# Second layer's weights and first x1 loaded during the first layer, last x1 stores not waited for, and statistics put ahead of the lane product

## What is computed

```python
x = _L0_conv_ref(x, Wk, bk, Wq, bq, Wv, bv, Wp, bp)      # x1, (8, 256, 48, 48)
x = _L1_conv_ref(x, w_qkv, w_dw, w_pw, w_proj, gamma, beta)

# layer 0
keys, queries, values = (conv1x1(x, W, b).reshape(n, 8, 32, hw) for W, b in ...)
context  = einsum('nhkp,nhvp->nhkv', softmax(keys, 3), values)
attended = einsum('nhkv,nhkp->nhvp', context, softmax(queries, 2))
x1 = conv1x1(attended.reshape(n, 256, h, w), Wp, bp) + x

# layer 1
qkv = einsum('oc,bchw->bohw', w_qkv, x1)                 # 768 channels
ms  = depthwise 5x5 (w_dw), then a grouped 8x8 product (w_pw), of qkv
q, k, v1 = relu, relu, v with a row of ones              # 64 heads of 8, of [qkv, ms]
out = (v1 k^T) q;  out = out[:-1] / (out[-1:] + 1e-15)
y   = einsum('oc,bchw->bohw', w_proj, out)
out = (y - mean) * rsqrt(var + 1e-5) * gamma + beta + x1  # mean, var over all images
```

## Time and profile before

| | us |
|---|---|
| median of 3 runs | 2305.25 (2300.67 to 2306.81) |
| profiled execution, its own time | 2298.37 |
| its span in the profile | 2296.6 |
| PE busy | 2063.2 (90%) |
| DVE busy | 1431.6 (62%) |
| ACT busy | 867.6 (38%) |
| POOL busy | 564.5 (25%) |
| DMA moved | 450.91 MB, mean 196 GB/s |

### The profile page before, as it was taken

One profiled execution on the slowest core, in us unless ns is written; L12 is line 12 of the kernel. 1 busy time (PEld: TensorE's weight loads), 2 busy tenths in 40 slices (PEclk: granted clock), 3 DMA queues, 4 the chain that ended last, 5 costly groups with the idle time before them and its releaser, 6 DMA issues. The chain is left out here.

```text
span 2296.6 us, 33675 instructions
## 1 busy us (share of the span) xinstructions
PE 2063.2 (90%) x13448; PEld 1517.2 (66%) x13448; DVE 1431.6 (62%) x2079; ACT 867.6 (38%) x1840; POOL 564.5 (25%) x483
## 2 busy tenths in 40 slices
PE   8999999999696999899989989999998998999810
PEld 7888889898574666566656656656765665666500
DVE  6667777667138765838757665784855659380452
ACT  5444444443443423433433332343343234333142
POOL 1223322231232222321322232232232223212000
PEclk9999999999897999999999999999999999999865
DMA  2221122200677756664775766567587567657578
GB/s 108 83 83 42 42 83 83 83 42 16 247 263 272 252 196 241 228 229 174 258 252 201 251 232 227 188 239 257 177 286 235 198 228 241 228 179 273 237 327 372
DMA packets 144475, 450.91 MB, mean 196 GB/s; under 512 B 7744, under 2 KB 106688, under 8 KB 120000
## 3 DMA queue, kind: packets, MB, share of 16 engines
q1 hardware_dynamic: 143168, 429.89, 52.6%
q10 hardware_dynamic: 1152, 18.87, 1.9%
HBM read 273.95 MB, written 174.78 MB: 195 GB/s over the span
## 5 line engine op out<-in xcount | busy, mean ns | idle before, releaser
L789 PE MATMUL cv<-work,wc 128*64 128x288 f32 x4608 | 630.2, 419 | 60.2 <-DMA work<-scratch_padded 45.1
L1147 POOL TENSOR_TENSOR wc<-taps 128x512 f32<-128x512 f32 x288 | 365.8, 1298 | 749.4 <-PE cv L789 739.3
L789 PEld LDWEIGHTS cv<-work,wc 128*64 128x64 f32 x4608 | 310.7, 138 | 306.8 <-issue 54.2
L1009 ACT ACTIVATE work<-cv 128x288 f32<-128x288 f32 x384 | 158.0, 411 | 535.1 <-PE cv L789 533.6
L1211 DVE STREAM_SHUFFLE spun<-work 128x1152 f32<-128x1152 f32 x240 | 346.8, 1451 | 0.1
L1217 DVE SCALAR_TENSOR_TENSOR spun<-work,spun 128x1152 f32<-128x1152 f32 x240 | 338.9, 1417 | 0.0
L768 PE MATMUL pj<-x1hi,w1hi 128*128 128x288 f32 x768 | 235.2, 306 | 27.1 <-DVE x1lo L1194 22.4
L990 ACT COPY work<-pj 128x288 f32<-128x288 f32 x384 | 154.4, 402 | 201.8 <-PE pj L770 201.6
L770 PE MATMUL pj<-x1hi,w1lo 128*128 128x288 f32 x768 | 228.0, 297 | 0.0
L769 PE MATMUL pj<-x1lo,w1hi 128*128 128x288 f32 x768 | 227.2, 296 | 0.0
L768 PEld LDWEIGHTS pj<-x1hi,w1hi 128*128 128x128 f32 x768 | 145.9, 190 | 49.4 <-issue 47.0
(11 more groups left out here) (124 smaller groups left out, 3521.3 us busy)
## 6 DMA issues: line engine op xcount, KB each, us to landing
work<-scratch_padded SPq DMA_DIRECT2D x48, 1306.0 KB, 6.8
scratch_padded<-work SPq DMA_DIRECT2D x48, 1300.0 KB, 7.2
work<-scratch_padded SPq DMA_DIRECT2D x48, 1299.5 KB, 10.2
scratch_phases<-work SPq DMA_DIRECT2D x96, 576.0 KB, 5.2
work<-scratch_phases SPq DMA_DIRECT2D x64, 576.0 KB, 6.0
x<-scratch_x SPq DMA_DIRECT2D x10, 2304.0 KB, 10.8
scratch_x<-xs SPq DMA_DIRECT2D x8, 2304.0 KB, 6.9
q<-scratch_phases SPq DMA_DIRECT2D x32, 576.0 KB, 5.4
```

The costliest lines, as they stand in the source:

```text
L789: mm = nc.tensor.matmul(cv[64 * b:64 * b + 64, j % 2, :PLANE], wc[:, 2 * j + b, dy].rearrange("p c o -> p (c o)"), window, start=(dy == 0) ...
L1009: nc.scalar.activation(stage[:, j // 4, j % 4], cv[:, j % 2, :PLANE], ACT.Copy if PARTS[u] == 2 else ACT.Relu).then_inc(cv_freed, 1)
L1147: op = nc.gpsimd.tensor_tensor(wc[:, blocks, dy], taps[:, u % 2, blocks, 0:DIM].rearrange("p g (c o) -> p g c o", o=1).to_broadcast([P, HB ...
```

## The change

It does two things.

1. The load of layer 1's projection weights goes into layer 0's SP stream, behind the load of x[1], into a place of its own at the top of SBUF (`wqkv1`). x1 of image 0 is loaded in layer 0 as well, once all queries and values of image 6 are made; it goes to `x1_first`, which is where `x1` will lie, and where `xhi` of the even images was. The waits for the last two x1 stores (`x_stored`) leave layer 0's end; instead SP waits for them in `lay_load` before the first load into `q`, and ACT in `copy_queries` of image 0, since `q` lies where `xs` was. Both weight casts are split: the 512 columns of units 0 and 1 first, the other 1024 after the pieces of x1.
2. In DVE's order, `statistics(i - 1, Y_CHUNKS[3])` goes ahead of `spin(i, 3)`.

```diff
-def phase_l0(nc, dram, sem):
+def phase_l0(nc, dram, sem, ahead, x_out):
...
             sp.dma_start(xs[:, 1], dram["x"][1]).then_inc(x_in[1], 16)
+            x1_first, wqkv1, x1_in, w1_in = ahead
+            sp.dma_start(wqkv1[:], dram["wqkv"]).then_inc(w1_in, 16)
...
+            sp.wait_ge(qv_filled, (NIMG - 1) * NPAIR)
+            sp.dma_start(x1_first[:], dram["x1"][0]).then_inc(x1_in, 16)
             for par in range(2):
                 n = NIMG - 2 + par
                 sp.wait_ge(x1_done, (n + 1) * NPAIR)
                 sp.dma_start(dram["x1"][n], xs[:, par]).then_inc(x_out[par], 16)
-            for par in range(2):
-                sp.wait_ge(x_out[par], 16 * NIMG // 2)
-
...
-            sp.dma_start(wqkv[:], dram["wqkv"]).then_inc(w_first, 16)
             for u in range(2):
                 sp.dma_start(taps[:, u], dram["taps"][u]).then_inc(taps_in[u], 16)
-            sp.dma_start(x1[:], dram["x1"][0]).then_inc(x_in, 16)
...
                 else:
+                    for stored in x_stored:
+                        sp.wait_ge(stored, 16 * NIMG // 2)
                     wait_count(sp, y_out, 16 * len(Y_CHUNKS) * i)
                     wait_count(sp, bn_done, 2 * NCH * i)
...
-            pe.wait_ge(w_split, 2)
-
             def project(i, u, chunks=range(NG)):
 
+                if i == 0 and chunks[0] == 0:
+                    pe.wait_ge(w_split if u < 2 else w_rest, 2)
...
-            nc.scalar.copy(whi[:], wqkv).then_inc(w_split, 1)
+            nc.scalar.copy(whi[:, :, 0:2], wqkv[:, :, 0:2]).then_inc(w_split, 1)
...
             for s in range(4):
                 high(0, s)
+            nc.scalar.copy(whi[:, :, 2:], wqkv[:, :, 2:]).then_inc(w_rest, 1)
...
+                if i == 0:
+                    for stored in x_stored:
+                        act.wait_ge(stored, 16 * NIMG // 2)
...
-            nc.vector.tensor_tensor(wlo[:], wqkv, whi[:].bitcast(F32), ALU.subtract).then_inc(w_split, 1)
+            nc.vector.tensor_tensor(wlo[:, :, 0:2], wqkv[:, :, 0:2], whi[:, :, 0:2].bitcast(F32), ALU.subtract).then_inc(w_split, 1)
...
             low(0, range(4))
+            dve.wait_ge(w_rest, 1)
+            nc.vector.tensor_tensor(wlo[:, :, 2:], wqkv[:, :, 2:], whi[:, :, 2:].bitcast(F32), ALU.subtract).then_inc(w_rest, 1)
...
                 if prev:
                     statistics(i - 1, Y_CHUNKS[2])
+                if prev:
+                    statistics(i - 1, Y_CHUNKS[3])
                 if i != last_image:
                     spin(i, 3, range(0, 6))
                     low(i + 1, range(4))
-                    spin(i, 3, range(6, 9))
-                if prev:
-                    statistics(i - 1, Y_CHUNKS[3])
-                if i != last_image:
-                    spin(i, 3, range(9, 16))
+                    spin(i, 3, range(6, 16))
```

More of the change, by code:

```diff
@@ L143, in mbank @@
             return kx[:, 1, 0:C] if h == 0 else qv[:, 2, 0:C]
-        (w_in, wkqv_in, w_hi, w_lo, x_in0, x_in1, x_out0, x_out1, hi_ready, lo_ready, k_filled, k_freed, nmax_ready, exp_done,
+        (w_in, wkqv_in, w_hi, w_lo, x_in0, x_in1, hi_ready, lo_ready, k_filled, k_freed, nmax_ready, exp_done,
          qv_filled, v_done, q_added, e_filled, e_freed, ctx_step, ctx_masked, rk_ready, m_filled, mthi_ready, mtlo_ready, qnlo_ready, q_maxed,
@@ L148, in phase_l0 @@
             sem(f"l0_{n}") for n in (
-                "w_in wkqv_in w_hi w_lo x_in0 x_in1 x_out0 x_out1 hi_ready lo_ready k_filled k_freed nmax_ready exp_done "
+                "w_in wkqv_in w_hi w_lo x_in0 x_in1 hi_ready lo_ready k_filled k_freed nmax_ready exp_done "
                 "qv_filled v_done q_added e_filled e_freed ctx_step ctx_masked rk_ready m_filled mthi_ready mtlo_ready qnlo_ready q_maxed "
                 "q_shifted q_exp q_summed q_recip q_ready x_filled x1_done").split())
-        x_in, x_out = (x_in0, x_in1), (x_out0, x_out1)
+        x_in = (x_in0, x_in1)
         NW = 5
@@ L527, in _, with phase_l1 @@
                     image(2 * it + par, par)
-def phase_l1(nc, dram, sem, bnst, q, x1, xhi, xlo, work, early, x_again):
+def phase_l1(nc, dram, sem, bnst, q, x1, xhi, xlo, work, early, x_again, ahead, x_stored):
     with ExitStack() as ctx:
@@ L554, in phase_l1 @@
         rcp = work[:, 4 * CT * HW + REST:4 * CT * HW + REST + 2 * CHUNK]
-        wqkv = kva.rearrange("p t n -> p (t n)")[:, 0:CT * NU * P].rearrange("p (k u m) -> p k u m", k=CT, u=NU)
+        x1_first, wqkv, x_in, w_first = ahead
         kvT = sb("kvT", [P, 2, 2, 2, P + 1])
@@ L572, in phase_l1 @@
         ao = ps("ao", [P, 512])
-        (w_in, w_first, taps_in0, taps_in1, x_in, zeroed, ones_set, wc_ready, pj_filled, pj_freed,
+        (w_in, taps_in0, taps_in1, zeroed, ones_set, wc_ready, pj_filled, pj_freed,
          padded_out0, padded_out1, cv_filled, cv_freed, lay_stored0, lay_stored1, lay_stored2, lay_stored3, lay_done0, lay_done1, lay_done2, lay_done3, spun_ready, spun_summed, vkd_ready, tr_filled, tr_freed, vk_step, vk_freed,
@@ L578, in phase_l1 @@
             sem(f"l1_{n}") for n in (
-                "w_in w_first taps_in0 taps_in1 x_in zeroed ones_set wc_ready pj_filled pj_freed "
+                "w_in taps_in0 taps_in1 zeroed ones_set wc_ready pj_filled pj_freed "
                 "padded_out0 padded_out1 cv_filled cv_freed lay_stored0 lay_stored1 lay_stored2 lay_stored3 lay_done0 lay_done1 lay_done2 lay_done3 spun_ready spun_summed vkd_ready tr_filled tr_freed vk_step vk_freed "
@@ L585, in phase_l1 @@
         rep_in = [sem(f"l1_rep_in{r}") for r in range(3)]
-        w_split, xhi_ready, xlo_ready = sem("l1_w_split"), sem("l1_xhi_ready"), sem("l1_xlo_ready")
+        w_split, w_rest, xhi_ready, xlo_ready = sem("l1_w_split"), sem("l1_w_rest"), sem("l1_xhi_ready"), sem("l1_xlo_ready")
         lay_stored, lay_done = ((lay_stored0, lay_stored1), (lay_stored2, lay_stored3)), ((lay_done0, lay_done1), (lay_done2, lay_done3))
@@ L964, in _ @@
             act.wait_ge(w_first, 16 * NFIRST)
-            nc.scalar.copy(whi[:], wqkv).then_inc(w_split, 1)
+            nc.scalar.copy(whi[:, :, 0:2], wqkv[:, :, 0:2]).then_inc(w_split, 1)
             def high(i, s):
                 act.wait_ge(x_in, 16 * (i + 1))
-                nc.scalar.copy(x_part(xhi, s), x_part(x1, s)).then_inc(xhi_ready, 1)
+                nc.scalar.copy(x_part(xhi, s), x_part(x1 if i else x1_first, s)).then_inc(xhi_ready, 1)
             for s in range(4):
                 high(0, s)
+            nc.scalar.copy(whi[:, :, 2:], wqkv[:, :, 2:]).then_inc(w_rest, 1)
             act.wait_ge(zeroed, 1)
@@ L1193, in low @@
                     dve.wait_ge(xhi_ready, 4 * i + s + 1)
-                    nc.vector.tensor_tensor(x_part(xlo, s), x_part(x1, s), x_part(xhi, s).bitcast(F32),
+                    nc.vector.tensor_tensor(x_part(xlo, s), x_part(x1 if i else x1_first, s), x_part(xhi, s).bitcast(F32),
                                             ALU.subtract).then_inc(xlo_ready, 1)
             low(0, range(4))
+            dve.wait_ge(w_rest, 1)
+            nc.vector.tensor_tensor(wlo[:, :, 2:], wqkv[:, :, 2:], whi[:, :, 2:].bitcast(F32), ALU.subtract).then_inc(w_rest, 1)
             def spin(i, p, share):
@@ L1393, in build @@
         bnst = ctx.enter_context(nc.sbuf_tensor("bnst", [P, CT, NIMG, NCH, 6], F32))
-        phase_l0(nc, dram, sem)
+        first = -(-nc.sbuf_base // 32) * 32
+        x1_first = nc.alloc_sbuf_tensor_at("x1_first", [P, CT, HW], F32, offset=first + 2 * CT * HW * 4)
+        wqkv = nc.alloc_sbuf_tensor_at("wqkv1", [P, CT, NU, P], F32, offset=nc.sbuf_top - CT * NU * P * 4)
+        ahead = (x1_first, wqkv, sem("l1_x_in"), sem("l1_w_first"))
+        x_stored = (sem("l0_x_out0"), sem("l0_x_out1"))
+        phase_l0(nc, dram, sem, ahead, x_stored)
         q = ctx.enter_context(nc.sbuf_tensor("q", [P, 4, HW], F32))
@@ L1405, in build @@
                  (y_third[:], None, sem("out_load3")))
-        phase_l1(nc, dram, sem, bnst, q, x1, xhi, xlo, work, early, x_again)
+        phase_l1(nc, dram, sem, bnst, q, x1, xhi, xlo, work, early, x_again, ahead, x_stored)
         phase_out(nc, dram, sem, bnst, q, x1, early, x_again)
```

## The result

| | before | after |
|---|---|---|
| median, us | 2303.42 (4 runs, 2300.67 to 2306.81) | 2273.40 (4 runs, 2269.61 to 2273.62) |
| ratio of the runs | | 0.9865, 95% interval 0.9847 to 0.9884 |
| profiled execution | 2298.37 | 2273.38 |
| its span | 2296.6 | 2271.6 |

On two later occasions before took 2301.3 (median of 15) and 2301.75 (median of 7); beside the latter the change took 2273.43, ratio 0.9879 (0.9864 to 0.9894). The change makes the kernel some 28 us faster.

A forecast was written before the change was run, and what follows sets the result against it. TensorE, busy 90% of the span, bounds the kernel, so only its idle waits yield time. The terms, -17 at the boundary and -5 from the statistics, make -22 us from the 2305.25 median: 2283 us, range 2274 to 2293.

The forecast's parts named there:

- Part 1: Layer boundary: without the store wait, with early loads and split casts, TensorE restarts at 576.1, 17.0 us earlier (14.5 to 17.4).
- a memset that holds nothing: Boundary: POOL's 4.58 us memset beside VectorE's low pieces delays nothing, so TensorE starts at 575.7, a gain of 17.4 us.
- the 0.4 us I added: Boundary: added to TensorE's start of 575.7 because low pieces beside POOL's tap products took 1.73 us each, shortest 1.35.
- Part 2: Statistics moved ahead: the padded copy's wait goes, a projection wait comes; 0.9 us gained per image, 5 us in all.
- The chain of delays: Image 2: lane product 6.8 us later, low at 1133.0, new 7.2 us projection wait, padded copy ready before TensorE wants it.
- another 1.4 us. So the wait is worth 8.9 us per image: Convolution behind the padded copy: 7.47 us standing plus 1.4 us from twelve matmuls at half clock, 3.07 instead of 1.68.
- the 0.2 us I took off for the other images: Image 2's gain of 1.1 us lowered to 0.9, as copies end 6.0 us behind the landing on the mean, 5.77 there.
- The starting point: The gain of 22 us was counted from 2305.25, the median of the runs shown, 7 us above the profiled execution's 2298.37.
- The six waits simply go: Rival 1, padded copy: low of x1 is never late, part 2 gives 53 us, total 2235; chance 3%.
- The crossing that holds for the store: Rival 2, boundary: engines still wait for the store and start at 579.0, TensorE 6.6 us later than forecast, 2290; chance 8%.
- POOL's products beside the lane product: Rival 3: a second POOL group delays the six steps by 3.12 us instead of 0.45; total 2299; chance 5%.
- The slower rival: Rival 4, next image's convolution 0: a padded store trip of 18.3 us leaves both waits standing, +31 us, 2336; chance 3%.

The follow-up runs named there:

- part 1 alone: The change with the old order of statistics (early loads, no wait for the x1 stores, split casts), against the kernel before: 2287.14 us, ratio 0.9931.
- part 2 alone: The kernel before with only the last statistics moved ahead of the lane product: 2290.29 us, ratio 0.9951.
- the wait alone: The change with all four last statistics behind low, but VectorE's wait for ScalarE's last copy kept ahead of the lane product: 2275.56 us, ratio 0.9889 to before.
- the wait put back: The change with the two waits for the x1 stores again at the first layer's end: 2279.80 us, ratio 0.9902 to before.
- the split statistics: The change with chunk 4's last statistics left ahead of the lane product and chunk 5's put behind low: 2237.25 us, ratio 0.9716 to before.

## Why the prediction was wrong

**Part 1 held.** Engines start: forecast 572.4, measured 572.1. Restart: 576.1 against 575.34. The end of the range taken for a memset that holds nothing was right, 575.7; the 0.4 us I added from the low pieces beside the tap products did not come. The rule of the Trainium skill (SBUF — State Buffer, section "SBUF: two separate sides"), by which a GpSimd operation that reads no SBUF holds no VectorE operation with two inputs, agrees with the trace: 1.35 us a piece beside the memset and behind it, against 2.21, the median of all pieces of before, which in image 2 run beside POOL's products. In the profiles the boundary gave 17.7 us against 17.0, in the runs of part 1 alone 15.9.

**Part 2 held in its mechanism and not in its size.** The chain of delays came as told: lane product at the last copy plus 0.6 us (I had 1.0), low 18.7 us on (18.6), a wait of 6.92 us (7.2, and 7.4 over the images), no wait at the convolution, no statistics wait on SP. The step that failed is its size, 5 us, and in it "another 1.4 us. So the wait is worth 8.9 us per image". The 1.4 is the loss of the first twelve matmuls of image 2. They take much the same in all six images, 3.07 or 3.15 us, as in image 3:

```profile
1356.49 3.15 PE L789 MATMUL cv<-work,wc 128*64 128x288 f32 x12 [7.78 <-DMA work<-scratch_padded]
```

What was left out is how long the half clock goes on behind them. The mean clock in the 8 us behind each of the six restarts of before, third number from the right, is

```profile
964.80:972.80 8.00, 8.00 (x46) 4.45 (x48) 2.45 (x2) 2.12 (x6) 0.67 (x2) 0.73 0.98 388
1160.79:1168.79 8.00, 8.00 (x50) 4.26 (x51) 2.51 (x2) 2.17 (x7) 0.67 (x2) 0.82 1.00 395
1356.49:1364.49 8.00, 8.00 (x42) 4.31 (x44) 2.21 (x2) 2.12 (x6) 0.67 (x2) 0.68 0.97 385
1553.31:1561.31 8.00, 8.00 (x49) 4.28 (x50) 2.13 (x2) 2.16 (x7) 0.67 (x2) 0.82 1.00 396
1748.75:1756.75 8.00, 8.00 (x42) 4.35 (x44) 2.48 (x2) 2.12 (x6) 0.67 (x2) 0.66 0.99 390
1944.78:1952.78 8.00, 8.00 (x48) 4.41 (x48) 3.02 (x4) 2.12 (x6) 0.67 (x2) 0.75 1.00 396
```

8 us at 0.82 lose 1.4 us, at 0.66 they lose 2.7. In image 2, which I used, it ends about with the twelve, and it is one of the two mildest; the mean loss is 2.0. The wait was worth 9.6 us per image, not 8.9. In after the restart at the projection loses 2.1 us in each, first and last row:

```profile
921.57:929.57 8.00, 8.00 (x45) 8.00 (x46) 7.96 (x10) 2.54 (x7) 0.00 (x0) 0.72 0.22 78
...
1894.59:1902.59 8.00, 8.00 (x46) 8.00 (x47) 7.96 (x10) 2.65 (x7) 0.00 (x0) 0.74 0.22 78
```

This lengthened the projection to 8.5 us (I had 8.0 from image 0). And the 0.2 us I took off for the other images, whose data landed earlier before the copies, was wrong: the restart in after hangs on TensorE's own output and ScalarE's copy, at the same distance in each image. Per image the profiles show 1.4 us, 8.4 in all, less 1.1 that image 0 lost: 7.3 us against my 5. Runs of part 2 alone say 11.3 (8.5 to 14.3). A part of that gap is the old wait itself: the 1.4 us per image rest on the first profile of before, whose images are the shortest of the three profiles with that wait, 196.0 us on the mean. With 196.2 and 196.6 of the other two, the same sum (six times the difference to 194.6, less 1.1) gives 8.5 and 10.9. That is an estimate; which executions are typical, three profiles do not say.

**The starting point was off by 4 us.** I set the gain off from 2305.25, the median of three runs. The median of fifteen is 2301.3: 4 us. The profiled execution of before, from which the terms came, was in turn 3 us faster than that, while that of after is at its own median; so the medians lie 28 us apart where the two profiles lie 25. With part 1's 0.7 and part 2's 2.3 us this makes 10, for the 9.6 us between 2283 and 2273.4. Counted by the runs it is the start 4.0, part 2 6.3 (11.3 against 5) and part 1 -1.1 (15.9 against 17), together 9.2. So by the runs part 2's size is the largest error, and the start the second. The range took the 3 us by which runs differ around the right sum, not around a start that was itself off. Its ends were also not added up alike: 2305 - 17.4 - 9 - 3 is 2275.6, but 2305 - 14.5 + 2 + 3 is 2295.5, not 2292.

**The rivals.** "The six waits simply go" was false for this change and true of a neighbour: with the statistics behind low it is what happens, 2226 us. What I had against it, that the copies end after the data, held, and the experiment with the wait alone shows that this wait is what stood against it. The crossing that holds for the store is excluded by the restart and by the kernel with the wait put back. POOL's products beside the lane product cost about what one more group was put at: low began 18.74 us behind the lane product's start, where 18.6 was forecast and 18.16 was measured with one group. In the kernel with the wait alone it was 19.30. The slower rival did not come near: the store left at 1125.30, the copy back could be issued at 1131.02, and the convolution that needs it, at 1143.45, 18.2 us behind the store, shows no wait.

Two things stay open: why the six restarts of one execution run between 2.9 and 5.4 us at half clock, and how much of the 3 us by which before's profile lay under its median belongs to the old wait. No single place holds them.

## What to carry to other kernels

When work is moved ahead in a queue that runs in order, look not at how long it takes but at what it waits for: four instructions of 2 us were free, and the copy they wait for cost 7 us per image, nearly all that their early end gave back. Look for the latest place that still serves the one who waits, here behind the urgent low half and 8 us ahead of where they were; it gave 47 us more than the earliest place. A cost that is read in one of six like places should be read in all six, and to its end: the first twelve matmuls looked alike in all of them.

## What was not expected of the hardware

After a wait of some 7.5 us TensorE stays at half clock, 1.2 GHz, for 2.9 to 5.4 us, in one execution, at places that are otherwise alike; it costs 1.4 to 2.7 us each. A memset of 4.58 us on POOL did not slow VectorE's subtractions (1.35 us each, 5.16 for four), whereas POOL's products of two inputs stretched four of them to 6.91 us in before and to 7.78 in the kernel with the split statistics.
